# A fused transformer block on one Trainium2 core: the second norm's scale and shift moved from VectorE to GpSimd, and one copy on ScalarE moved ahead of the normalisations

## What is computed

```
mod = silu(c) @ wmod                        # six vectors of 128 per batch: sa, ca, ga, sb, cb, gb
ga, gb: magnitude at least 0.25, sign kept
h = layernorm(x) * (1 + ca) + sa
q, k, v = split(h @ w_attn); q, k = elu(.) + 1      # 16 heads of 8
y_t = (q_t @ sum_{s<=t} k_s v_s^T) / (q_t . sum_{s<=t} k_s + 1e-6)
x = x + ga * (y @ w_proj)
h = layernorm(x) * (1 + cb) + sb            # the second norm
e = argmax(h @ Wg + bg)                     # one of 8 experts per token
x = x + gb * (gelu(h @ W1[e]) @ W2[e])      # 128 -> 512 -> 128
```

## Time and profile before

| | |
|---|---|
| median of 3 runs | 343.55 us |
| lowest, highest run | 339.87, 344.41 us |
| span of the profiled execution | 339.4 us |
| attention loop, a step | 24.70 us |
| step 7 (no front) | 18.51 us |
| PE busy in the span | 285.0 us |
| DVE, ACT, POOL busy | 241.9, 152.0, 124.8 us |

### The profile page before, as it was taken

How to read it: one execution, slowest core, us unless ns; L and a number is a source line. 1 busy time by engine, 2 the same in 40 slices (tenths; PEclk the granted TensorE clock), 3 DMA queues, 4 the chain that set the end, 5 groups by cost and what they waited for, 6 DMA issues and landing times.

```text
span 339.4 us, 10754 instructions
## 1 busy us (share of the span) xinstructions
PE 285.0 (84%) x3847; PEld 245.5 (72%) x3847; DVE 241.9 (71%) x842; ACT 152.0 (45%) x301; POOL 124.8 (37%) x142
## 2 busy tenths in 40 slices
PE   1777989999999999999999998942129999999980
PEld 1446678688688788787787887742119999999980
DVE  4974557778778778778687787663735888988880
ACT  3378491780871871861952830000023444444430
POOL 8979000303503404305305205232311546545662
PEclk9997999999999999999999999785558999999995
DMA  7990000001000001001001001000252334333410
GB/s 212 319 302 5 3 2 2 2 3 35 34 4 37 27 0 48 16 0 63 1 0 64 0 0 66 2 34 33 82 162 70 108 90 117 93 95 97 113 38 0
DMA packets 16906, 20.19 MB, mean 59 GB/s; under 512 B 2747, under 2 KB 13117, under 8 KB 16882
## 3 DMA queue, kind: packets, MB, share of 16 engines
q1 hardware_dynamic: 13040, 12.50, 13.1%
q0 software_dynamic: 2832, 6.57, 5.6%
q10 hardware_dynamic: 1010, 0.81, 0.8%
HBM read 12.22 MB, written 8.10 MB: 60 GB/s over the span
## 4 chain that ended last, share of the span: by engine, by line
PE 63%; DVE 15%; issue 6%; ACT 4%; POOL 3%; DMA 3%; DVEq 2%; SPq 1%; POOLq 0%; ACTq 0%
PE bank L1001 18%; PE bank L1013 5%; PE bank L1138 5%; PE bank L1147 4%; PE bank L1033 4%; PE bank L1020 4%; PE bank L956 3%; DVE k_q L885 3%; PE bank L1062 3%; PE bank L979 2%; PE bank L971 2%; ACT h_t L432 2%; POOL sorted_rows L374 2%; PE bank L962 2%; PE bank L1047 2%
## 5 line engine op out<-in xcount | busy, mean ns | idle before, releaser
L374 POOL DMA_INDIRECT sorted_rows<-row_buf,slot_i x32 | 31.6, 987 | 119.7 <-DVE slot_i L777 112.4
L1001 PE MATMUL bank<-q_m,k_q 128*64 128x128 f32 x1024 | 71.9, 284 | 2.6 <-DVE probs L654 2.0
L654 DVE TENSOR_TENSOR probs<-bank,causal 128x256 f32<-128x256 f32 x128 | 51.6, 421 | 22.8 <-PE bank L1001 21.9
L1001 PEld LDWEIGHTS bank<-q_m,k_q 128*64 128x64 f32 x1024 | 56.2, 140 | 10.5 <-DVE probs L654 5.9
L396 POOL DMA_INDIRECT out_dram<-q_m,slot_token x39 | 40.8, 1047 | 44.9 <-DVE q_m L901 27.1
L1138 PE MATMUL bank<-q_m,k_q 128*128 128x128 f32 x312 | 43.0, 283 | 0.0
L1147 PE MATMUL bank<-k_q,v_m 128*128 128x128 f32 x312 | 41.5, 276 | 0.0
L1138 PEld LDWEIGHTS bank<-q_m,k_q 128*128 128x128 f32 x312 | 39.6, 199 | 0.0
L1147 PEld LDWEIGHTS bank<-k_q,v_m 128*128 128x128 f32 x312 | 38.1, 193 | 0.4 <-DVE q_m L898 0.4
L541 ACT ACTIVATE v_m<-bank 128x512 f32<-128x512 f32 x39 | 23.3, 598 | 27.2 <-PE bank L1138 27.2
L484 ACT ACTIVATE rden<-bank 128x512 f32<-128x512 f32 x8 | 4.8, 597 | 49.7 <-PE bank L987 49.6
(11 more groups left out here) (177 smaller groups left out, 510.6 us busy)
## 6 DMA issues: line engine op xcount, KB each, us to landing
v_m<-sorted_rows SPq DMA_DIRECT2D x39, 132.0 KB, 2.1
x_all<-in_L_attn_x_dram SPq DMA_DIRECT2D x16, 128.0 KB, 4.2
w_all<-in_L_ffn_W_dram SPq DMA_DIRECT2D x1, 2048.0 KB, 9.6
out_dram<-q_m,slot_token POOLq DMA_INDIRECT x39, 2.3
sorted_rows<-zeros ACTq DMA_DIRECT2D x4, 132.0 KB, 2.3
sorted_rows<-zeros SPq DMA_DIRECT2D x4, 132.0 KB, 2.5
sorted_rows<-row_buf,slot_i POOLq DMA_INDIRECT x32, 2.4
wmod_sb<-in_L_wmod_dram SPq DMA_DIRECT2D x1, 384.0 KB, 4.8
```

Of the source, the lines that this page charges most:

```text
L374: pool.indirect_dma_start(sorted_rows, bass.IndirectOffsetOnAxis(ap=slot_i[par][:, t:t + 1], axis=0), row_buf[par][:, t, :], None).then_in ...
L654: V.tensor_tensor(probs[:, s, b, q, :], score_bank[q % 2][:, 0:QUADS * L], causal[:].rearrange("p a t -> p (a t)"), ALU.mult).then_inc(pro ...
L1001: last = mm(score_bank[q % 2][L * half:L * half + L, 2 * L * n:2 * L * n + 2 * L], k_q[par][:, q, tok:tok + L], q_m[par][:, 2 * half:2 * h ...
```

## The change

GpSimd's `route_norm` gets two more products behind its own two: h2 times (1 + cb) and h2 plus sb, each over 128 partitions and 512 elements, each waiting for the one before (`plain_ready`, the new `scaled`) and for the gates; the second raises `h2_ready`. DVE's `route_modulate` leaves the loop and remains for the last group only, where it also still does the norm. On ScalarE `route_turned(g - 1)` moves from behind `front_norm(f + 1)` to ahead of it.

```
@@ gpsimd: route_norm
                 nc.gpsimd.tensor_tensor(h2, h2, rstd2[:].unsqueeze(2).broadcast_to([P, GT, C]), ALU.mult
                                         ).then_inc(plain_ready, 1)
+                by_batch = h2.rearrange("p (b s) c -> p b s c", b=B)
+                pool.wait_ge(gates_ready, 1)
+                pool.wait_ge(plain_ready, ready)
+                nc.gpsimd.tensor_tensor(by_batch, by_batch, mod_bc[:, :, 2, :].unsqueeze(2).broadcast_to([P, B, 2, C]),
+                                        ALU.mult).then_inc(scaled, 1)
+                pool.wait_ge(gates_ready, 1)
+                pool.wait_ge(scaled, ready)
+                nc.gpsimd.tensor_tensor(by_batch, by_batch, mod_bc[:, :, 1, :].unsqueeze(2).broadcast_to([P, B, 2, C]),
+                                        ALU.add).then_inc(h2_ready, 1)
@@ scalar: step
                     front_kn(f, fpar)
+                if route:
+                    route_turned(g - 1)
                 if norm:
                     front_norm(f + 1)
-                if route:
-                    route_turned(g - 1)
                 if front:
                     masked_q(f, fpar)
@@ vector: route_modulate, step
-            def route_modulate(r, par, chain, norm=False):
-                if norm:
-                    for t in range(GT):
...
-                else:
-                    dve.wait_ge(plain_ready, r + 1)
+            def route_modulate(r, par, chain):
+                for t in range(GT):
...
                 core_y(g, par, 1)
-                if route:
-                    route_modulate(g - 1, 1 - par, chain)
                 core_probs(g, 1, 1, FIRST)
```

More of the change, by code:

```diff
@@ L210, in build @@
         proj_mm, x1_ready = sem("proj_mm"), sem("x1_ready")
-        var2_ready, guess2_ready, norm2_ready, centred, plain_ready = (
-            sem(n) for n in ("var2_ready", "guess2_ready", "norm2_ready", "centred", "plain_ready"))
+        var2_ready, guess2_ready, norm2_ready, centred, plain_ready, scaled = (
+            sem(n) for n in ("var2_ready", "guess2_ready", "norm2_ready", "centred", "plain_ready", "scaled"))
         h2_ready, h2t_mm, h2t_ready, logit_mm, onehot_ready, rank_mm, slots_ready = (
@@ L699, in route_newton @@
                 newton(rstd2[:], guess2[:], newton2[:], var2[:], chain).then_inc(norm2_ready, 1)
-            def route_modulate(r, par, chain, norm=False):
-                if norm:
-                    for t in range(GT):
-                        last = V.tensor_scalar(row_buf[par][:, t, 0:C], row_buf[par][:, t, C:2 * C],
-                                               mean2[:, t:t + 1], rstd2[:, t:t + 1], ALU.subtract, ALU.mult)
-                    chain.link(last)
-                else:
-                    dve.wait_ge(plain_ready, r + 1)
+            def route_modulate(r, par, chain):
+                for t in range(GT):
+                    last = V.tensor_scalar(row_buf[par][:, t, 0:C], row_buf[par][:, t, C:2 * C],
+                                           mean2[:, t:t + 1], rstd2[:, t:t + 1], ALU.subtract, ALU.mult)
+                chain.link(last)
                 h2 = row_buf[par][:, :, 0:C].rearrange("p (b s) c -> p b s c", b=B)
@@ L777, in rden_and_slots @@
                     V.tensor_copy(slot_i[par][:], slot_f[:]).then_inc(slots_ready, 1)
-            LINKS = 3 + 3 + 1 + 7 + 7
+            LINKS = 3 + 3 + 7 + 7
             def step(g, par, turn, chain, front=True, route=True):
@@ L840, in _ @@
             dve.wait_ge(norm2_ready, G)
-            route_modulate(G - 1, 1, chain, norm=True)
+            route_modulate(G - 1, 1, chain)
             z_and_argmax(G, 0, G - 1, chain, False, True)
```

## The result

The changed kernel takes 368.12 us in the median of four runs (362.26 to 371.84), against 343.41 us for the kernel before (339.87 to 344.41, four runs). The forecast was 350.0 us, range 345 to 356, within 2% slightly more likely than slower. The time lies outside the range. The profiled execution is the lowest of the four, 362.26 us at a granted clock of 0.886; the other three, without a trace, took 365.08, 371.16 and 371.84 us at 0.878, 0.865 and 0.857, so the longer ones most likely had more of the half clock that the trace shows.

The account below looks back on a forecast made before the run. The prediction took PE (TensorE) to bound the loop, busy 24.14 of 24.70 us per step. The GpSimd move cost 0 and five PE stalls of 1.30 us added 6.5 to the median 343.55: 350.0 us, range 345 to 356.

Parts of the forecast that it names:

- PE is the bound, and only what PE waits for counts: Attention loop: PE busy 24.14 of 24.70 us per step, so taking 1.4 us off DVE in seven steps gains 0.
- A product on GpSimd takes 1.26 us and hides: Scale and shift on GpSimd: 1.26 us per product, inside a hole before the scatter, so cost 0.
- The tight place in step 7: Last step: h2 from GpSimd at 217.4, wanted by PE at 218.12; forecast 0, bound +0.9 us once.
- The stall is 1.30 us, in five steps: Steps 1 to 5: PE waits 1.30 us for q_m, queued behind copy and xhat on ScalarE.
- The walk through step 6: Next to last step, without xhat: copy 0.69 us after the transposes' start, next instruction 0.63 later, used to time the stall.
- The sum is 5 x 1.30 = 6.5 us: Whole loop: five stalls of PE add 6.5 us (5.75 to 7.5), everything else 0.
- The price of the clock: Rival, 22%: each stall also halves PE's clock; 5 x 2.8 = 14 us if all do, 357.5 us.
- the one case seen before: Last step: after PE idles 1.52 us the clock is 0.50 from 212.93 to 216.00, losing 1.5 us.
- stands alone in a busy step: Argument against the clock falling: the 1.30 us stall of PE is isolated in an otherwise busy loop step.
- a gap of 1.37 us in the start: At 23.75, after PE's gap, 32 matmuls took 1.15 us as at full clock; argued against clock loss.
- The number: Whole kernel: median 343.55 + 6.5 = 350.0 us, +1.9%.
- The other sum, 339.4 + 6.5: Whole kernel: the profiled execution's span of 339.4 us plus the stalls' 6.5 gives 345.9 us.

Follow-up runs that it names:

- e1: Changed kernel with ScalarE's order of before, so only scale and shift are on GpSimd: 357.65 us against 358.78 for the kernel before, ratio 0.996.
- e9: Kernel before with only the copy moved ahead of the normalisations on ScalarE: 369.43 us against 339.93 before, ratio 1.083.
- e5: The changed kernel itself, measured again in a later set: 363.24 us against 340.6 for the kernel before, ratio 1.056.
- e2: Kernel before with only the copy moved ahead of the normalisations, on the first chip: 371.55 us against 358.78 before, ratio 1.039.
- e8: Changed kernel with one of the four xhat ahead of the copy on ScalarE and three behind: 353.63 us, ratio 1.032 to the kernel before.
- e11: Kernel before with matmuls on constants keeping PE busy behind the loop: 339.45 us against 339.93 before, ratio 0.994.
- e6: Changed kernel with eight constant transposes on PE ahead of the scores in steps 1 to 6: 351.44 us against 340.6 before, ratio 1.033.
- e7: Changed kernel with two of the four xhat ahead of the copy on ScalarE and two behind: 345.46 us, ratio 1.013 to the kernel before.
- e10: Changed kernel with ScalarE's order copy, q_m, xhat: 344.13 us against 339.93 for the kernel before, ratio 1.008.
- e12: Changed kernel in ScalarE's order copy, q_m, xhat, plus constant matmuls on PE behind the loop: 343.75 us, ratio 1.010 to the kernel before.
- e3: Changed kernel with eight constant transposes on PE ahead of the scores in steps 1 to 6, first chip: 366.47 us against 358.78 before, ratio 1.017.

## Why the prediction was wrong

Point by point, in its own order:

- *PE is the bound, and only what PE waits for counts.* Right. 1.37 us less of DVE in seven steps gave nothing (e1), and DVE's wait behind it grew to 2.39 us.
- *A product on GpSimd takes 1.26 us and hides.* Right in price (1.27, beside 1.04 for the products with an operand broadcast along the row) and cover. The tight place in step 7 was priced at 0 with a bound of 0.9 and measures 0.79, at the price forecast: PE came there earlier, since the clock had not fallen behind its 1.51 us wait, as it had in the earlier trace rows.
- *The stall is 1.30 us, in five steps.* Right: 1.26, five times. The walk through step 6, where the copy already stood without xhat in front, gave the starts of the copy and of xhat within 0.01 us. q_m came 0.12 us earlier than reckoned (step 2: the transposes start at 100.09, q_m at 102.97), and PE started 0.13 instead of 0.04 us after q_m's end; that these two nearly cancel is luck. Nothing gave the stall back: PE's waits of 0.33 to 0.42 us for h_t stand in the loop as before.
- *The sum is 5 x 1.30 = 6.5 us.* **This step failed.** It took the stall as costing only itself. The price of the clock stood among the rivals with 22%, and there it was too low as well: 1.5 us per fall from the one case seen before, against 15.49 us for five, 3.1 each. In the trace before, the half clock lasted 3.4 us at its one place in the loop; behind the new waits it lasted 3.4 to 10.2 us, and in e9 13.7, though PE was busy all that time.
- *The reason given against it* was that the stall "stands alone in a busy step" and that a gap of 1.37 us in the start had not cost clock. The first was no protection: the clock fell behind five of five waits of 1.26 us in the changed kernel's profile and in e9's, four of five in e5's and three of five in e2's. The gap in the start was one case among several. PE in the kernel before, 5 us later:

```profile
28.77 1.12 PE L987 MATMUL bank<-ident,qz 128*128 128x128 f32 x4 [1.54 <-DVE qz L769]
```

  Its transposes take 1.12 us instead of 0.66, so this gap was followed by half clock, as the 1.52 us in the earlier trace rows was. With both beside the one that was read, the rival would have stood at even odds or more.
- *Whether a wait brings the clock down is not set by its length alone,* which the prediction's one case could not tell. The wait of 1.51 to 1.52 us in step 7 stands in ten of the traces, and the half clock follows it in three: before, e8 and e9. In e11, whose loop is that of the kernel before, it does not:

```profile
214.51 1.09 PE L1001 MATMUL bank<-q_m,k_q 128*64 128x128 f32 x16 [1.51 <-DVE probs L654]
```

- *The Trainium skill's rule* (TensorE: Matmul & The Clock Gate, Part 1) is that how busy PE has recently been sets its clock. e6 agrees: with 48 useless transposes the clock is 1.00 behind all five waits for q_m, and the time is 11.8 us under the changed kernel's by the medians.
- *The number* was taken from the median, 343.55 + 6.5, which stands by itself. The other sum, 339.4 + 6.5, mixes two measures: in every run that lists both, the time is 1.7 to 1.85 us above the span, so the profiled execution before took about 341.2 us by this estimate, and not 339.87.

That the clock falls because PE idles is shown (e6 and e7 against e5). That the reorder is the whole cause is shown (e1, e2, e9). What decides whether the clock falls behind a given wait, and how long the half clock then lasts, from 3.4 to 13.7 us behind the same wait of 1.26, is open.

## What to carry to other kernels

Where PE is the bound and runs without gaps, waits of 0.7 to 1.3 us cost 2 to 4 us each here (by the ratios e8 lost 10.8 us for five of 0.73, e5 18.9 for five of 1.26): price each new wait of PE with the clock it may lose, and look for every place where the trace already shows the half clock, not for one: how often it follows a wait and for how long. Before moving an instruction that waits, list what is queued behind it and how much slack the engine that needs it has: here 0.2 us. With q_m ahead of xhat (e10) it is 0.34, not the 2 us that e12's expectation names, and that is enough. If PE must wait in a stage that it bounds, matmuls on constants into an unread bank can cost less than the clock they keep (e6); behind the loop they gave about 2 us (e11).

## What the runs showed of the hardware

The same kernel before took 358.8 us on one chip and 339.9 and 340.6 on others. In the traces from that slower chip PE and DVE wait at the turns of the loop with no engine to wait for. PE in e1 and e3:

```profile
168.40 1.75 PE L1005 MATMUL bank<-q_m,k_q 128*64 128x128 f32 x16 [3.36 <-issue]
```

```profile
116.24 1.09 PE L1005 MATMUL bank<-q_m,k_q 128*64 128x128 f32 x16 [2.93 <-issue]
```

The instruction queue moves more packets in those traces than in the changed kernel's own first one. e1, then the changed kernel:

```profile
q8 instruction: 24, 0.39, 0.5%
```

```profile
q8 instruction: 15, 0.25, 0.3%
```

e10, on another chip, has 24 too and a single such wait, and so has e6. The half clock follows some of these waits and not others: in e3 it does not follow the one above, of 2.93 us. That these are waits for instructions to be loaded is a reading of these rows, not shown: no trace of the kernel before was taken there. It is why only ratios on one chip are used above.
